# Group normalisation, attention and a displacing convolution on one core: a group chain in two sets and weights transposed by pair of heads

## The reference

```python
# layer 0
h   = group_norm(x, 32 groups)                    # over 24 channels x 1024 positions
qkv = h_tokens @ W_qkv.T                          # 12 heads of 64
s   = var(v) @ var(k).T * 64 ** -0.5              # variances over a head's 64 values: an outer product
out = softmax(s) @ v
x   = x + (out @ W_proj.T + b_proj)
# layer 1
g   = group_norm(x, 32 groups)
x   = x + depthwise3x3(shift(g, offset), exp kernels of offset)   # shift per 16 channels, zeros come in
```

## Time and profile before

| | |
|---|---|
| runs of before | 2065.40, 2065.43, 2069.72 us; median 2065.43 |
| the profiled execution | 2068.55 us, its span 2066.8 us |
| TensorE busy | 2002.8 us (97%) |
| VectorE busy | 1668.6 us (81%) |
| ScalarE busy | 1207.0 us (58%) |
| GpSimd busy | 264.3 us (13%) |
| instructions | 33759 |

### The profile page before, as it was taken

The page is one execution under the profiler, slowest core; times in us unless marked ns, Lnnn a source line. Parts: engine busy times, 40 slices in busy tenths (PEclk is TensorE's granted clock), DMA queues, the critical chain, the costliest instruction groups (busy, mean ns, idle before and its releaser), DMA issues.

```text
span 2066.8 us, 33759 instructions
## 1 busy us (share of the span) xinstructions
PE 2002.8 (97%) x12924; PEld 1115.2 (54%) x12924; DVE 1668.6 (81%) x3594; ACT 1207.0 (58%) x1321; POOL 264.3 (13%) x323
## 2 busy tenths in 40 slices
PE   3999999999999999999999999999999999999997
PEld 3756347662565536554376634766256553655443
DVE  6688576997679976898769987699867997699857
ACT  3576734776267743778527783477626774377820
POOL 2100001111012100111001210111101210011121
PEclk9999999999999999999999999999999999999998
DMA  8212303445044541446114561344603454144514
GB/s 324 83 53 63 103 1 102 133 130 180 2 124 144 162 116 42 126 129 205 45 63 126 158 178 22 99 130 133 184 2 124 144 162 116 42 128 132 147 35 183
DMA packets 104978, 236.33 MB, mean 114 GB/s; under 512 B 46704, under 2 KB 47472, under 8 KB 104816
## 3 DMA queue, kind: packets, MB, share of 16 engines
q0 software_dynamic: 31968, 116.41, 19.4%
q1 hardware_dynamic: 66800, 95.74, 15.3%
q10 hardware_dynamic: 6048, 22.02, 3.1%
HBM read 154.06 MB, written 79.73 MB: 113 GB/s over the span
## 4 chain that ended last, share of the span: by engine, by line
PE 58%; DVE 20%; DMA 8%; issue 7%; ACT 5%; SPq 1%; ACTq 0%; POOL 0%; DVEq 0%; POOLq 0%
PE ps L1303 23%; PE ps L1360 16%; PE ps L1345 14%; DVE bt L885 7%; ACT ring L671 5%; DVE st L837 3%; DMA a_sb<-a_rows 3%; PE ps L1320 2%; DMA dt_sb<-d_sb 2%; DMA a_rows<-at 1%; DVE bst_x L811 1%; DMA bt<-r_rows 1%; DVE bt L1008 1%; DVE bt L1005 1%; SPq L447 1%
## 5 line engine op out<-in xcount | busy, mean ns | idle before, releaser
L671 ACT ACTIVATE ring<-a_sb,coef 128x1024 f32<-128x1024 f32 x768 | 817.7, 1137 | 23.5 <-issue 12.3
L1303 PE MATMUL ps<-wkv_hi,h_sp 128*128 128x256 f16 x4608 | 771.8, 273 | 3.9 <-DVE h_sp L828 2.4
L1345 PE MATMUL ps<-ring,xv 128*64 128x512 f32 x3072 | 691.3, 597 | 6.2 <-ACT ring L671 5.1
L1303 PE MATMUL ps<-wkv_lo,h_sp 128*128 128x256 f16 x2304 | 628.8, 273 | 0.0
L885 DVE TENSOR_TENSOR bt<-bt,ring 128x1024 f32<-128x1024 f32 x464 | 541.8, 1212 | 3.0 <-ACT ring L671 1.7
L1303 PEld LDWEIGHTS ps<-wkv_hi,h_sp 128*128 128x128 f16 x4608 | 451.5, 98 | 85.5 <-issue 28.5
L1345 PEld LDWEIGHTS ps<-ring,xv 128*64 128x64 f32 x3072 | 207.7, 137 | 427.0 <-issue 385.1
L655 ACT ACTIVATE xv<-ps 128x256 f32<-128x256 f32 x192 | 72.7, 383 | 511.8 <-DVE st L837 510.9
L1360 PE MATMUL ps<-xv,wp_hi 128*128 128x512 f16 x1152 | 349.7, 380 | 0.0
L837 DVE BATCH_NORM_STATS2 st<-ps 128x6 f32<-128x64 f32 x1536 | 217.0, 211 | 123.4 <-PE ps L1303 122.6
L1303 PEld LDWEIGHTS ps<-wkv_lo,h_sp 128*128 128x128 f16 x2304 | 225.7, 98 | 26.6
(11 more groups left out here) (164 smaller groups left out, 1397.9 us busy)
## 6 DMA issues: line engine op xcount, KB each, us to landing
a_sb<-a_rows SPq DMA_DIRECT2D x96, 512.0 KB, 5.4
out<-xv POOLq DMA_DIRECT2D x84, 512.0 KB, 5.3
xv<-in_x POOLq DMA_DIRECT2D x48, 512.0 KB, 3.7
h_sp<-in_x ACTq DMA_DIRECT2D x42, 512.0 KB, 5.3
shift_rows<-bt POOLq DMA_DIRECT2D x42, 512.0 KB, 3.4
bt<-r_rows SPq DMA_DIRECT2D x80, 256.0 KB, 4.0
shift_rows<-ring SPq DMA_DIRECT2D x12, 528.0 KB, 15.3
xv<-in_L_conv_W_qkv SPq DMA_DIRECT2D x4, 1152.0 KB, 14.2
```

What stands on the lines that cost most here:

```text
L671: nc.scalar.activation(ring_of(p, s, m), a_sb[:, h % 4, :], ACT.Exp, scale=coef[:, h, m:m + 1]).then_inc(s_exp, 1)
L1303: last = nc.tensor.matmul(ps[:, kv_bank[u % 2], half * 2 * P:(half + 1) * 2 * P], h_sp[:, k, hp, m * P:(m + 1) * P], wkv[wpart][:, k, q * ...
L1345: last = nc.tensor.matmul(ps[s * HD:(s + 1) * HD, o_bank[p % 2] + j, :], v_sb[:, p, m, s * HD:(s + 1) * HD], ring_of(p, s, m)[:, j * HALF: ...
```

## The change

1. The group chain of x runs in two sets of three tiles. The first is aggregated, averaged and squared while the second is still being read; each set has its own power, bias, and normalised tiles. The bias (rb_x's second column) is now a product on GpSimd, of the power and of the negated mean that VectorE leaves in `xneg`. GpSimd normalises one tile of each set (1 and 4), ScalarE two.
2. W_qkv is loaded in three parts, each the k and v rows of two pairs of heads, by two DMAs each. The maxima (now three, of 3072 columns) stand on VectorE between the steps of the group chain, ahead of the second set's epsilon.
3. An all-reduce over a constant is put on GpSimd ahead of the chain; the real one of W_qkv stands between the two sets.
4. A weight unit is now one block row (k or v of one pair of heads) and three channel tiles, so two units complete k and two more v of a pair. Four units are made before the first projection; behind the six projection units of phase A follow 6, 6, 5, 5, 5 and 5. The first projection waits for 4 low parts, unit 4 (the second pair) for 8.

The zeros are stored behind all loads in both kernels; that code is the same.

```diff
@@ w_unit
-        W_ORDER = (0, 2, 1, 3)
-        W_ROW = {1: 0, 3: 3, 0: 6, 2: 9}
-        Y_POOL = (1, 3, 5)
+        THIRD = KV // P * C // 3
+        W_FIRST = 4
+        W_SIDE = (6, 6, 5, 5, 5, 5)
+        Y_POOL = (1, 4)
...
+            g, kh = divmod(u, 2)
+            ks = slice(3 * kh, 3 * kh + 3)
             if u < WKU:
...
+                q, kind = divmod(g, 2)
+                lo = q * 2 * P + kind * P
+                return [w[:, ks, lo:lo + P] for w in wkv], scale[:, 0:1], wkv_nat[:, w_row(q, kind), :], 3 * kh, bank
@@ GpSimd, first()
                 pool.wait_ge(s_const, 5)
-                pool.wait_ge(s_xeps, 1)
-                nc.gpsimd.tensor_tensor(rb["x"][:, :, 0], xeps, mhalf_x, ALU.pow).then_inc(s_xpow, 1)
-                pool.wait_ge(s_xrb, 1)
-                for t in Y_POOL:
+                nc.gpsimd.partition_all_reduce(wmax_all[1], ones[:, 0:2], P, ABSMAX).then_inc(s_wall, 1)
+                for hh in (0, 1):
+                    cut = slice(3 * hh, 3 * hh + 3)
+                    if hh:
+                        pool.wait_ge(s_wmax, 3)
+                        nc.gpsimd.partition_all_reduce(wmax_all[0], wmax[0], P, ABSMAX).then_inc(s_wall, 1)
+                    pool.wait_ge(s_xeps, hh + 1)
+                    nc.gpsimd.tensor_tensor(rb["x"][:, cut, 0], xeps[:, cut], mhalf_x[:, cut], ALU.pow).then_inc(s_xpow, 1)
+                    pool.wait_ge(s_xpow, hh + 1)
+                    nc.gpsimd.tensor_tensor(rb["x"][:, cut, 1], rb["x"][:, cut, 0], xneg[:, cut], ALU.mult).then_inc(s_xrb, 1)
+                    pool.wait_ge(s_xrb, hh + 1)
+                    t = Y_POOL[hh]
                     nc.gpsimd.tensor_scalar(y_t[t], x_in[:, t, :], rb["x"][:, t, 0:1], rb["x"][:, t, 1:2],
                                             ALU.mult, ALU.add).then_inc(s_hfp, 1)
-                for n in (0, 1):
-                    pool.wait_ge(s_wmax, 4 + 2 * n)
-                    nc.gpsimd.partition_all_reduce(wmax_all[n], wmax[n], P, ABSMAX).then_inc(s_wall, 1)
+                pool.wait_ge(s_wmax, 5)
+                nc.gpsimd.partition_all_reduce(wmax_all[1], wmax[1], P, ABSMAX).then_inc(s_wall, 1)
@@ VectorE, first()
+                x_stats(0, range(3))
+                x_aggregate(0)
+                x_stats(0, range(3, CT))
+                x_aggregate(1)
+                x_spread(0)
+                third_max(0)
+                x_spread(1)
+                third_max(1)
+                x_var(0)
+                third_max(2)
+                x_var(1)
+                for t in range(3):
+                    h_second(0, t)
+                weights_scale(0)
                 h_second(0, 3)
-                weights_scale(0)
-                for u in range(2):
+                for u in range(W_FIRST // 2):
                     weight_second(u)
                 h_second(0, 4)
-                for u in range(2, 4):
-                    weight_second(u)
                 h_second(0, 5)
-                for u in range(4, WKU // 2):
+                for u in range(W_FIRST // 2, W_FIRST):
                     weight_second(u)
@@ ScalarE, VectorE and TensorE, beside_a(u)
-                for w in range(WKU // 2 + 4 * u, WKU // 2 + 4 * u + 4):
+                for w in w_beside(u):
...
@@ TensorE, kv_unit
-                    pe.wait_ge(s_wlo, WKU // 2)
+                    pe.wait_ge(s_wlo, W_FIRST)
+                if not later and halves[0] == 0 and u == UQ:
+                    pe.wait_ge(s_wlo, 2 * W_FIRST)
```

More of the change, by code:

```diff
@@ L198, in gn_attention_displace @@
         ps_at = ps[0:2 * MT, 7, 0:P]
-        s_wkv_in = [sem(f"s_wkv_in{n}") for n in range(4)]
+        s_wkv_in = [sem(f"s_wkv_in{n}") for n in range(3)]
         s_wp_in = sem("s_wp_in")
@@ L344, in gn_attention_displace, with w_row, w_beside @@
         WKU = KV // P * CT // 3
-        QUARTER = KV // P * C // 4
-        W_ORDER = (0, 2, 1, 3)
-        W_ROW = {1: 0, 3: 3, 0: 6, 2: 9}
-        Y_POOL = (1, 3, 5)
+        THIRD = KV // P * C // 3
+        W_FIRST = 4
+        W_SIDE = (6, 6, 5, 5, 5, 5)
+        Y_POOL = (1, 4)
+        def w_row(q, kind):
+            return 8 + 2 * q + kind if q < 2 else 2 * (q - 2) + kind
+        def w_beside(u):
+            lo = W_FIRST + sum(W_SIDE[:u])
+            return range(lo, lo + W_SIDE[u])
         def w_unit(u):
             bank = ps[:, 2 + u % 4, 0:3 * P].rearrange("p (q c) -> p q c", c=P)
+            g, kh = divmod(u, 2)
+            ks = slice(3 * kh, 3 * kh + 3)
             if u < WKU:
[L354 to L360, removed]
+                q, kind = divmod(g, 2)
+                lo = q * 2 * P + kind * P
+                return [w[:, ks, lo:lo + P] for w in wkv], scale[:, 0:1], wkv_nat[:, w_row(q, kind), :], 3 * kh, bank
+            t = g - WKU // 2
+            return [w[:, ks, t * P:(t + 1) * P] for w in wp], scale[:, 1:2], wp_nat[:, t, :], 3 * kh, bank
         GCH = 6
@@ L485, in first @@
                     sp.dma_start(x_in[:, t, :], x_t[0, :, t, :]).then_inc(s_xin[t], 16)
[L486 to L489, removed]
+                for n in range(3):
+                    at_ = (8, 0, 4)[n]
+                    for kind in (0, 1):
+                        row = (2 * C, C)[kind] + n * 2 * P
+                        sp.dma_start(wkv_nat[:, at_:at_ + 4, :].rearrange("p (q two) c -> p q two c", two=2)[:, :, kind, :],
+                                     w_qkv[row:row + 2 * P, :].rearrange("(q p) c -> p q c", p=P)).then_inc(s_wkv_in[n], 16)
                 sp.dma_start(wp_nat, w_proj.rearrange("(r p) c -> p r c", p=P)).then_inc(s_wp_in, 16)
@@ L1465, in transpose_weights @@
             def transpose_weights(u):
-                parts, sc, nat, k, r, bank = w_unit(u)
-                for q in range(3):
-                    last = nc.tensor.transpose(bank[:, q, :], nat[:, r + q, k * P:(k + 1) * P], ident[:, :])
+                parts, sc, nat, k, bank = w_unit(u)
+                for j in range(3):
+                    last = nc.tensor.transpose(bank[:, j, :], nat[:, (k + j) * P:(k + j + 1) * P], ident[:, :])
                 last.then_inc(s_wt, 1)
             def beside_a(u):
-                for w in range(WKU // 2 + 4 * u, WKU // 2 + 4 * u + 4):
-                    if w < WKU and w % CT == 0:
-                        pe.wait_ge(s_wkv_in[w // CT], 16)
+                for w in w_beside(u):
+                    if w < WKU:
+                        pe.wait_ge(s_wkv_in[w // 8], 32)
                     if w == WKU:
```

111 lines of the change are left out of this document (55 added, 56 removed).

## The result

The changed kernel took 2087.67 us in the median of 4 runs (2084.93 to 2093.47), the kernel before 2067.57 us beside it (4 runs, 2065.40 to 2070.52): a ratio of 1.0103, 95% interval 1.0084 to 1.0123. It is slower, by about 20 us (17 to 25 by the interval). That the median lies within 0.4 us of the forecast is partly luck: the four runs alone spread over 8.5 us. The profiled execution took 2089.68 us, its span 2087.9.

The account below looks back on a forecast made before the run. TensorE, 97% busy, was taken to bound the kernel, so set-up delay moves the end one for one; +4.4 up to the first projection and +17.5 behind it gave +21.9, 2087.3 us, range 2069 to 2095.5.

Parts of the forecast that it names:

- Half one: Set-up up to the first projection: GpSimd's switches outweigh the work taken out, start at 58.0 us, +4.4 us.
- With 8.6: GpSimd in the set-up: each switch between all-reduce and ordinary operations takes 8.6 us.
- The sum of +15: Whole kernel, if each GpSimd switch took about 6 us by the skill's rule: +15 instead of +21.9.
- Half two: First projection to first weighing: projections beside the remaining weight units, with bank waits and lower clock, +17.5 us.
- the unit with kmx: Transpose of the variances: the new gap lets VectorE catch up, 1.3 of the wait and the clock's fall go, -3.0.
- lower clock in units 0, 1, 2: TensorE's first projections: cold start and long gaps give two to three stretches at 1.2 GHz, +4.5 us.
- Edits at nothing: Six W_qkv DMA issues instead of four, the zeros' place and the switch before w_proj's all-reduce cost nothing.
- A: GpSimd in the set-up: shorter switches of 7.0 us, +17.5, 2083 us; chance 0.20.
- C: GpSimd in the set-up: only the way to the all-reduce costs, the way back is free, +12, 2077 us; chance 0.08.
- B: GpSimd in the set-up: switches free (0.3 us), as at the affine_select, +4.9, 2070.3 us; chance 0.17.
- D: Faster: free switches, gaps between projections half as long, no fall of the clock, 2061.5 us; chance 0.05.
- E: GpSimd switches over 9.7 us under the stream of loads: over +26, over 2091 us; chance 0.07.

Follow-up runs that it names:

- experiment 1: Changed kernel without the warm-up all-reduce over a constant: 2083.33 us, ratio 1.0074 to the kernel before.
- experiment 2: Changed kernel without the warm-up all-reduce and with W_qkv's all-reduce behind both sets: 2078.31 us, ratio 1.0050 to the kernel before.
- experiment 9: Kernel before with only the variances moved ahead of the weight units beside the same projection on VectorE: 2064.35 us, ratio 0.9981.
- 7: As experiment 6, with tile 4 normalised on ScalarE, variances ahead of weight units, their transpose waiting for 24 low parts: 2057.20 us, ratio 0.9956.
- 8: As 7, with 42 needless TensorE transposes ahead of the first projection: 2054.99 us, ratio 0.9946 to the kernel before.
- Experiment 4: Changed kernel with six PSUM banks for the weight units instead of four: 2076.01 us, ratio 1.0032 to the kernel before.
- experiment 6: Changed kernel with W_qkv's all-reduce behind both sets, no warm-up, six banks, last h copies ahead of first high parts: 2059.92 us, ratio 0.9973.
- experiment 3: Changed kernel with twelve weight units ahead of the first projection and four behind each: 2075.00 us, ratio 1.0050 to the kernel before.
- 5: Changed kernel with 42 needless TensorE transposes behind the second rb_x: 2088.87 us, ratio 1.0108 to the kernel before.

## Why the prediction was right, and where it was not

**What bounds the kernel.** Right in sum: 22.2 us at the first weighing, 22.2 at the next image's statistics, 21.1 at the end, with a drift between 17.7 and 23.9 on the way. Forecast were 21.9. That it came so close is luck in part: the two halves were off by 1.2 and 1.5 us in opposite directions, and the sizes inside the first by more.

**Half one, +4.4; measured +3.2.** The mechanism was right: GpSimd pays at every turn, in both directions, and the last two before the second rb_x lie on the path; experiments 1 and 2 show it. The second rb_x was forecast for 47.9 and came at 46.7; from there to the first projection 10.1 us were forecast and 10.1 measured. But two sizes inside were off, in opposite directions. "With 8.6" is not one number: the first two turns, beside the loads, took 10.5 and 11.0 us, the later two 6.0 and 7.7. My sentence that the first two "cost only 1 us", because the first variance was late anyway, was wrong: the variance was ready at 22.9 and the power started at 28.95, so they cost 6 us (in experiment 1 the power starts 6.6 us earlier). The two on the path cost 13.7 us, not 17.2. Power and product were 0.90 and 0.19 us, where I had 1.4 and 0.5. The errors cancelled to 1.2 us. The 2.39 us of the all-reduce at 40.74, which I had read as a sign of late code, came back only in experiment 9, which has GpSimd's order of before. In the changed order, right behind a turn, the all-reduce took 0.37 to 0.40 us, and 0.66 and 0.68 in 7 and 8, where it lay beside VectorE's subtractions, as it did before. So neither late code nor VectorE beside it accounts for it; the rest stays unexplained.

The Trainium skill's rule (GPSIMD Engine Reference, Instruction dispatch: about 6 us at the first call to freshly loaded code, with no instruction in the profile) is met in size by the turns to W_qkv's all-reduce, 5.8 to 6.3 us in the changed kernel and experiments 1 to 8; that they are the loading of code no run shows. The sum of +15, with 6 us at each turn, missed mainly because the first two took over 10 us, which delayed the first power by 6, and because the way back on the path took 7.7.

**Half two, +17.5; measured +19.0** (62.55 us from 56.78 to 119.33, against 43.56). By the starts in TensorE's timeline:

| term | forecast | measured |
|---|---|---|
| gaps behind projections 0 and 1 (now 5.4, 5.7 us) | +8.0 | +8.5 |
| gaps behind 2 to 5 (3.5, 3.3, 3.3, 3.3) | +8.0 | +8.0 |
| the unit with kmx (7.9 us, now 4.7) | -3.0 | -3.2 |
| lower clock in units 0, 1, 2 (2.7, 1.7, 1.3) | +4.5 | +5.7 |

Three terms stand within half a microsecond. The clock was under-sized: I took two to three falls, and the first unit ran slow for longer than a fall; TensorE came to it from 31.5 us of idling. The size of that 2.7 us is in part the luck of one execution: in the changed kernel and experiments 1, 2, 4, 6 and 7 the first unit took 5.2 to 6.9 us, and with twelve units ahead of it 3.9 (before), 3.9 (experiment 3) and 5.8 (experiment 9). Experiment 4 says what the gaps are: with two more banks they shrink to the transposes' own time, and the falls go with them.

**Edits at nothing.** The two more loads, the zeros' place and the turn ahead of w_proj's all-reduce cost nothing that the traces show; no run tested them alone. w_proj's all-reduce starts at 78.36, behind its operand, as forecast.

**Rivals.** My sums for A and C were 0.2 and about 1 us too low (17.5 with 4.4 less 4.2 is 17.7, and with 4.4 less 8.9 it is 13.0). A (turns of 7 us) was near for the two on the path, 13.7 for 14.0 us, but wrong for those under the loads. B and C (free turns, free way back) are excluded by experiments 1 and 2. The 0.3 us at the affine_select, on which B rested, was no measure of these turns; why that bare row is cheap, no run shows. D, faster, needed free turns and half the gaps. That it can be had, by one turn and six banks, is shown by 6 to 8. E (over 9.7 us) came true for the two turns beside the loads alone; the two on the path were shorter than forecast, so the sum stayed below E's +26.

**What the parts are worth.** Counted at the first weighing of the changed kernel (119.3 us): without the warm-up all-reduce -9.0 us, with the other one behind both sets too -10.5, with six banks alone -15.9, with twelve units ahead -15.5. Of the last two some 1.5 us aren't the edit's, since GpSimd's second rb_x came that much earlier there by the same code. The medians of the whole kernel fell by less: 4.3, 9.4, 11.7 and 12.7 us. The idea of the change, the maxima beside the group chain and weights by pair of heads, does bring the first projection forward, to 41.6 us in experiment 6 instead of 53.6, once rb_x waits for no turn.

## What to carry to other kernels

Group GpSimd's work by kind. Each turn between a partition all-reduce and ordinary operations, either way, cost 6 to 11 us here; the trace hides it under any longer wait, and it appears as "issue" once another engine no longer covers it. A "warm-up" call between ordinary operations pays two turns and saves none.

When work is moved from ahead of a loop into its gaps, count it against the buffers of the ring: behind a ring of four the fifth and sixth unit wait for a consumer, everything behind them on the same in-order engine waits too, and behind the longest gaps here the matmuls ran at the lower clock as well.

A gain that comes only since another wait grew longer is gone when that wait is repaired: look for it again (here, kmx).

## What the runs showed of the hardware that was not expected

- The price of a turn depends on the moment: 9.7 to 11.0 us where they lay within 7 to 29 us, beside the loads, in the changed kernel and in experiments 3, 4 and 5; 5.8 to 6.3 us to the all-reduce where it starts behind 31 us, and 6.9 to 7.7 us back. Busy DMA engines alone aren't the reason: they were as busy beside a turn of 11.0 us as beside one of 6.0 (changed kernel, windows inside the two turns; length and POOL busy with count, TensorE's clock, DMA share, GB/s), and experiment 1's turn of 6.3 us began at 24.8 us already. The cause stays open.

```profile
18.00:28.00 10.00, 0.00 (x0) 1.00 1.03 402
32.00:37.00 5.00, 0.00 (x0) 1.00 1.02 415
```

- The record of the granted clock says 1.00 until its first change, and in that time a projection unit took 6.6 us in the changed kernel and 3.9 us with transposes ahead of it; where the record has an earlier change, as in experiment 2, it says 0.50 for this unit. Early in a kernel the clock is to be read from the durations of matmuls. The Trainium skill (TensorE: Matmul & The Clock Gate, Part 1) says that the number of slow matmuls at the start differs between runs of one kernel; experiment 9 beside the kernel before agrees, with 5.8 and 3.9 us for the same unit after the same instructions.
- GpSimd beside VectorE's two-operand subtractions: 3.09 us for 1.19, and 1.05 for 0.19.
